# A two-layer conditioned transformer on one core: another order of the work in layer 1's attention, and in the turn from MLP 0 into it

## The chip, the cores and the metric

One Trainium2 chip, one of its cores. The metric is the device time of one execution in microseconds (us); the kernel before has a median of 254.11 us over 3 runs (253.97 to 254.25).

## The reference, cut to what matters

128 sequences of 32 rows, 128 features, float32. Two layers, each an attention and an MLP (128 to 512 to 128, exact gelu), both conditioned on a vector per sequence. Layer 0 has 16 heads, a layernorm, and a gate per sequence on what each half adds to the rows. Layer 1, which the change is about, has one head:

```python
h = film(rmsnorm(x, norm1_w), cond, film1_w, film1_b)     # x * (1 + scale) + shift, per sequence
Q, K, V = h @ q_w + q_b, h @ k_w + k_b, h @ v_w + v_b
attn = softmax(einsum("bnd,bmd->bnm", Q, K) * D ** -0.5)
x = x + (einsum("bnm,bmd->bnd", attn, V) @ proj_w + proj_b)
x = x + mlp(film(rmsnorm(x, norm2_w), ...))
```

The last step of MLP 0 is `x = x + gate_mlp * h`.

## The kernel before, in words

The 4096 rows lie as 32 tiles of 128 rows in the tile `X` of the on-chip memory. The work goes in 8 groups (`NG`) of 4 tiles: a group is 512 rows, 16 whole sequences. There are four phases of 8 groups: attention 0, MLP 0, attention 1, MLP 1. A running number `gg = phase * 8 + g` names a group in a phase: 16 to 23 are attention 1, 24 to 31 MLP 1. Most buffers are double and are picked by `p = g % 2`.

The order on each engine is written out by hand, a list per engine; the engines meet by counting semaphores (`wait_ge(sem, n)`), and each engine works its own list strictly in order. `group_steps` writes a step for the first one or two groups, then a hardware loop of two groups a turn, then the rest.

The chain of one group `gg` before its products:

- the statistics: in attention 1 ScalarE squares the rows (`sum_squares`), GpSimd raises to the power -1/2 (`power1`, L459) and scales the rows (`scale_rows`, L452) into `xhat`. For group 18, and in the MLPs, VectorE makes the statistics, GpSimd `power` (L338, L340) and ScalarE `apply` (L818).
- `rows_T` on TensorE (L1032) transposes 4 tiles of `xhat` into a PSUM bank; `modulate` on VectorE (L555) multiplies by the scale into `hA`; `add_shift` on GpSimd (L351) adds the shift into `h`. In attention 1 this last one also waits until the scores of the group two back are done (`s1_ready`), since these read the same buffer.

The products of group g of attention 1 on TensorE: `queries1` (L1282, h times the folded q/k matrix), `rows1` (L1288, V with the projection folded in, and a column of row terms), `scores1` (L1297, 16 products of 32 columns), `values1` (L1313, P times V into `y_ps`). Between them ScalarE moves the queries (`move_q1`, L1004) and takes the exponentials (`exps1`, L984); VectorE takes maxima and biases (`softmax1`, L650 to L655), moves V (`move_v1`, L674), divides and transposes P (`normalise1`, L660, L662, L667) and adds the product to the rows (`update(2, g)`, L567). `update(2, 0)` waits until `x_updated` is 17, which is reached when MLP 0's last group has been added to its rows.

MLP 0's group g ends so: `down` (L1275, 32 matmuls) into `y_ps`; VectorE adds the bias (`update(1, g)`, L564) into the single tile `yG`; GpSimd multiplies by the gate (L374) and adds to `X` (L376), both in `add_gated`. The product of MLP 0's last group, `down(1, 7)`, stands in TensorE's list behind the first products of attention 1.

TensorE's order before, in attention 1 (numbers are groups):

```
g = 0:     queries 0, rows 0, down(1,7), rows_T 18, scores 0, queries 1
g = 1..7:  rows g, scores g, queries g+1, (wait for P, V of g-1), rows_T g+18, values g-1
```

VectorE's: in a turn `softmax1(g)`, `move_v1(g)`, `modulate(g+18)`, `normalise1(g)`, `update(2, g-1)`. GpSimd's: `scale_rows(g+19)`, `add_shift(g+18)`, `power1(g+20)`, with `add_gated(1, 7)` in the turn of g = 0.

Of the kernel before, what the change touches and what calls it, by code (L numbers as in the profile page):

```python
# [17 lines left out]
ALU = mybir.AluOpType  # L18
ACT = mybir.ActivationFunctionType
# [11 lines left out]
TG = 4  # L31
NG = NT // TG
# [26 lines left out]
def build(nc, x, cond, weights, columns, rows, out):  # L59
    with ExitStack() as ctx:  # L60
# [9 lines left out]
        X = sb("X", [P, NT, D])  # L70
# [33 lines left out]
        eps1 = sb("eps1", [P, 1])  # L104
# [69 lines left out]
        def by_tile(ap):  # L174
            return ap.rearrange("p (t d) -> p t d", t=TG)
# [151 lines left out]
        def _(pool):  # L327
# [35 lines left out]
            def keep(phase, g, p):  # L363
# [2 lines left out]
                wait(pool, x_updated, gg)  # L366
                pool.tensor_tensor(by_tile(xg[:, p, :]), X[:, x_group(g), :], biases(phase), ALU.add).then_inc(xg_ready, 1)

            def add_gated(phase, g):

                gg = phase * NG + g
                pool.wait_ge(y_used, gg + 2)
                at = x_group(g) if isinstance(g, int) else bass.ds((gg + NG) % NG * TG, TG)
                pool.tensor_tensor(by_tile(yG[:, :]), by_tile(yG[:, :]), gate[:, phase, at, :], ALU.mult).then_inc(xg_ready, 1)  # L374
                pool.wait_ge(xg_ready, gg + 1)
                pool.tensor_tensor(X[:, at, :], X[:, at, :], by_tile(yG[:, :]), ALU.add).then_inc(x_updated, 1)  # L376

            def add_shift_half(half):
                if half == 0:
# [64 lines left out]
            def scale_rows(gg, p):  # L444

                pool.wait_ge(rstd_ready, gg + 1)
                if isinstance(gg, int) and gg == 2 * NG + 3:
                    pool.wait_ge(hT_ready, gg)
                else:
                    pool.wait_ge(hT_ready, gg - 1)  # L450
                at = x_group(gg % NG) if isinstance(gg, int) else bass.ds(gg % NG * TG, TG)
                pool.tensor_tensor(by_tile(xhat[:, p, :]), X[:, at, :],  # L452
                                   rstd[:, p, :].unsqueeze(2).broadcast_to([P, TG, D]), ALU.mult).then_inc(xhat_ready, 1)

            def power1(gg, p):

                pool.wait_ge(v_ready, gg + 1)
                wait(pool, xhat_ready, gg - 1)
                pool.tensor_tensor(rstd[:, p, :], v_sb[:, p, :], minus_half[:, :], ALU.pow).then_inc(rstd_ready, 1)  # L459

            def attention1(g, p):
                scale_rows(2 * NG + g + 3, 1 - p)
                add_shift(2 * NG + g + 2, p, 2, g)
                if isinstance(g, int) and g == 0:
                    add_gated(1, 7)
                if known(g, 0, NG - 1):
                    power1(2 * NG + g + 4, p)

            def mlp(phase):
                def step(g, p):  # L470
                    gg = phase * NG + g
                    first = isinstance(g, int) and g == 0
                    if phase == 1 and first:
                        power(gg + 3, 1 - p)
                        add_shift(gg + 2, p, phase, g)
                        pool.wait_ge(gates_in[0], 16 * NG)
                        add_gated(0, 7)
                        return
                    if phase == 1 or known(g, 0, 6):
                        add_shift(gg + 2, p, phase, g)  # L480
                    if phase == 1:
                        power(gg + 3, 1 - p)
                    elif known(g, 0, 5):
                        power(gg + 3, 1 - p, NG)
                    if phase == 1:
                        if p == 1:
                            pool.wait_ge(gates_in[1], 8 * (g + 1))
                        add_gated(1, g - 1)
                    else:
                        keep(phase, g, p)  # L490
                return step

            group_steps(pool, attention0)
            group_steps(pool, mlp(1))
            power1(2 * NG + 3, 1)
            group_steps(pool, attention1, first=2, turns=2)
            group_steps(pool, mlp(3), turns=2)


        @block.vector  # L500
        def _(dve):
# [268 lines left out]
            def attention1(g, p):  # L770
                first = isinstance(g, int) and g == 0
                if first:
                    move_v1(g, p)
                    update(1, 7, 1)
                    modulate(2 * NG + g + 2, p)
                    softmax1(g)
                    normalise1(g, p)
                    return
                softmax1(g)
                move_v1(g, p)  # L780
                modulate(2 * NG + g + 2, p)
                normalise1(g, p)
                update(2, g - 1, 1 - p)

            group_steps(dve, attention0)
            group_steps(dve, mlp(1))
            group_steps(dve, attention1, first=2)
            group_steps(dve, mlp(3), turns=2)
            dve.wait_ge(xg_ready, 3 * NG)
            for half in range(2):  # L790
# [7 lines left out]
        def _(act):  # L798
# [205 lines left out]
                act.activation(Qs[:, p, :], bank[2][:, :], ACT.Identity, bias=wqk[:, D + 1:D + 2]).then_inc(q1_moved, 1)  # L1004

            def attention1(g, p):
                if known(g, 0, NG - 1):
                    sum_squares(2 * NG + g + 4, p, range(TG))
                exps1(g, p)
                if known(g, 0, NG - 1):  # L1010
                    move_q1(g + 1, 1 - p)

            group_steps(act, mlp(1))
            sum_squares(2 * NG + 3, 1, range(TG))
            act.wait_ge(wqk_copied, 1)
            move_q1(0, 0)
            group_steps(act, attention1, first=2, turns=2)
            group_steps(act, mlp(3), turns=2)


        @block.tensor
        def _(pe):
# [299 lines left out]
            def mlp(phase):  # L1322
                def step(g, p):
                    gg = phase * NG + g
                    first = isinstance(g, int) and g == 0
                    if first and phase == 1:
                        rows_T(NG + 2, 0)
                        up(1, 1, 1, (0,))
                        output_T(7, 1)
                        up(1, 1, 1, (1,))  # L1330
                        project0(7, 1)
                        up(1, 1, 1, (2, 3))
                        return
                    elif first:
                        pe.wait_ge(v1_moved, NG)
                        pe.wait_ge(bias1_ready, NG)
                        pe.wait_ge(wmlp1_in, 16)
                        up(phase, g, p)
                    elif not (phase == 1 and isinstance(g, int) and g == 1):
                        up(phase, g, p)  # L1340
                    else:
                        fold_qk()
                    if phase < 3 or not isinstance(g, int) or g < 6:
                        rows_T(gg + 2, p)
                    if not first:
                        down(phase, g - 1, 1 - p)
                    elif phase == 3:
                        wait_values1(7)
                        values1(1)
                return step  # L1350

            def attention1(g, p):
                first = isinstance(g, int) and g == 0
                if first:
                    pe.wait_ge(g_ready, NC * NG)
                    pe.wait_ge(wqk_copied, 1)
                    queries1(g, p)
                rows1(g, p)
                if first:
                    down(1, 7, 1)  # L1360
                    rows_T(2 * NG + g + 2, p)
                scores1(g, p)
                if known(g, 0, NG - 1):
                    queries1(g + 1, 1 - p)
                if not first:
                    wait_values1(g - 1)
                    rows_T(2 * NG + g + 2, p)
                    values1(1 - p)

            group_steps(pe, mlp(1), first=2)  # L1370
            group_steps(pe, attention1, first=2, turns=2)
# [47 lines left out]
```

## Time and profile before

| what | value |
|---|---|
| median of 3 runs | 254.11 us |
| the profiled execution's own time | 254.23 us |
| its span, first to last instruction | 252.4 us |
| TensorE (PE) matmuls busy | 239.5 us, 95% |
| VectorE (DVE) | 162.8 us, 65% |
| ScalarE (ACT) | 156.8 us, 62% |
| GpSimd (POOL) | 154.2 us, 61% |
| mean granted TensorE clock | 0.999 |
| attention 0, with the start | 0 to about 96 us |
| MLP 0 | about 96 to 153.7 us |
| attention 1 | 153.7 to 189.1 us |
| MLP 1 | 189.1 to 252.4 us |

PE is busy in nearly the whole span, so the time is that of PE's list plus the holes in it. Float32 products go through PE in passes, so `queries1` shows as 2 matmuls and `rows1` as 8. The profile's own 1.8 us between span and time lie around the program.

### The profile page before, as it was taken

Reading aid. Unit: us, or ns where it says so; the run is one execution under the profiler, and the core shown is the slowest. Engines: PE = TensorE matmul, PEld = TensorE weight load, DVE = VectorE, ACT = ScalarE, POOL = GpSimd, SP = SyncE. Lnnn points to the kernel's source line nnn. Section 1 sums busy time; section 2 is a strip of 40 time slices with the busy share of each in tenths; the row PEclk is TensorE's granted clock in tenths of the full one; section 3 lists DMA queues with packets and bytes.
Section 4 is the critical chain, followed back from the end, with each engine's and each line's share of the span. In section 5 each row is a group of like instructions: output and inputs, shape, how many; then the busy total and the mean of one; then the engine's idle time right before and its main releaser. Section 6 shows DMA issues by size and latency. Waiting matters only on the chain.

```text
span 252.4 us, 9860 instructions
## 1 busy us (share of the span) xinstructions
PE 239.5 (95%) x3727; PEld 181.0 (72%) x3727; DVE 162.8 (65%) x507; ACT 156.8 (62%) x396; POOL 154.2 (61%) x173
## 2 busy tenths in 40 slices
PE   5899879999999989999999999899999999999995
PEld 5676667787877866766778669677775766677775
DVE  7898888988989997455554543578888354442102
ACT  5469867866966849745445666887856666443340
POOL 4486846585685778677656667788784544554120
PEclk9999999999999999999999999999999999999999
DMA  6943334325256222412100000000000011110112
GB/s 192 326 127 91 122 128 116 122 65 164 94 145 206 104 76 71 134 62 75 71 12 0 0 0 0 4 3 4 0 4 0 0 44 42 42 29 14 44 42 83
DMA packets 17163, 18.01 MB, mean 71 GB/s; under 512 B 1648, under 2 KB 12656, under 8 KB 17136
## 3 DMA queue, kind: packets, MB, share of 16 engines
q1 hardware_dynamic: 16272, 15.41, 20.0%
q10 hardware_dynamic: 864, 2.24, 2.8%
q8 instruction: 17, 0.28, 0.6%
q14 instruction: 10, 0.08, 0.1%
HBM read 11.48 MB, written 4.59 MB: 64 GB/s over the span
## 4 chain that ended last, share of the span: by engine, by line
PE 80%; DVE 4%; POOL 4%; issue 4%; DMA 2%; SPq 2%; ACT 2%; POOLq 0%; ACTq 0%; DVEq 0%
PE bank L1275 23%; PE bank L1064 10%; PE pair L1064 10%; PE bank L1032 5%; PE bank L1142 5%; PE pair L1112 4%; PE bank L1124 3%; PE bank L1163 3%; PE pair L1288 3%; PE pair L1079 2%; PE bank L1071 2%; PE bank L1282 2%; PE bank L1313 2%; PE bank L1112 2%; PE bank L1092 2%
## 5 line engine op out<-in xcount | busy, mean ns | idle before, releaser
L818 ACT ACTIVATE xhat<-X,shift,rstd 128x128 f32 (+1 forms) x88 | 36.9, 487 | 41.1 <-POOL shift L340 41.1
L1275 PE MATMUL bank<-W,Kx 128*128 128x128 f32 x512 | 59.6, 275 | 0.0
L1275 PEld LDWEIGHTS bank<-W,Kx 128*128 128x128 f32 x512 | 58.5, 192 | 1.0 <-issue 1.0
L351 POOL TENSOR_TENSOR h<-hA,B 128x512 f32<-128x512 f32 x31 | 32.5, 1048 | 32.6 <-DVE hA L555 32.4
L555 DVE TENSOR_TENSOR hA<-bank,A 128x512 f32<-128x512 f32 x31 | 21.1, 681 | 32.9 <-PE bank L1032 17.7
L1064 PE MATMUL bank<-h,W 128*128 128x512 f32 x62 | 32.0, 597 | 0.1
L338 POOL TENSOR_TENSOR rstd<-v_sb,minus_half 128x4 f32<-128x4 f32 x24 | 24.5, 1020 | 10.9 <-DVE v_sb L540 5.8
L1064 PE MATMUL pair<-h,W 128*128 128x512 f32 x62 | 29.4, 592 | 0.0
L359 POOL TENSOR_TENSOR Ss<-Sc,smax 128x512 f32<-128x512 f32 x16 | 16.8, 1050 | 18.9 <-DVE smax L581 18.8
L896 ACT ACTIVATE Kx<-bank,col 128x512 f32<-128x512 f32 x32 | 21.7, 677 | 8.1 <-PE bank L1064 8.1
L1032 PEld LDWEIGHTS bank<-ident,xhat 128*128 128x128 f32 x124 | 15.0, 142 | 14.8 <-issue 12.9
L374 POOL TENSOR_TENSOR yG<-yG,gate 128x512 f32<-128x512 f32 x16 | 20.3, 1271 | 7.9 <-DVE yG L564 6.8
L376 POOL TENSOR_TENSOR X<-X,yG 128x512 f32 (+1 forms) x16 | 20.4, 1272 | 2.4 <-POOL yG L374 2.1
L873 ACT ACTIVATE Sc<-bank 128x512 f32<-128x512 f32 x16 | 9.6, 599 | 19.0 <-PE bank L1112 18.1
L1064 PEld LDWEIGHTS pair<-h,W 128*128 128x128 f32 x62 | 11.5, 190 | 13.4 <-issue 13.4
L896 ACT ACTIVATE Kx<-pair,col 128x512 f32<-128x512 f32 x32 | 20.3, 676 | 0.7 <-PE pair L1064 0.7
L526 DVE BATCH_NORM_STATS2 stats<-X 128x6 f32 (+1 forms) x96 | 20.6, 277 | 0.1
L1032 PE MATMUL bank<-ident,xhat 128*128 128x128 f32 x124 | 18.9, 275 | 0.5 <-ACT xhat L818 0.3
L564 DVE TENSOR_TENSOR yG<-bank,row 128x512 f32<-128x512 f32 x16 | 10.8, 676 | 11.9 <-PE bank L1275 9.2
L1142 PE MATMUL bank<-Vx,PT 128*32 128x36 f32 x1024 | 14.8, 200 | 3.8 <-DMA Kx<-Ks 1.2
L1142 PEld LDWEIGHTS bank<-Vx,PT 128*32 128x32 f32 x1024 | 12.2, 109 | 8.6 <-issue 5.5
L1112 PE MATMUL bank<-Kx,Qs 32*32 32x128 f32 x512 | 18.2, 273 | 0.0
(155 smaller groups left out, 467.3 us busy)
## 6 DMA issues: line engine op xcount, KB each, us to landing
values_scratch<-Vs SPq DMA_DIRECT2D x8, 288.0 KB, 2.1
Vx<-values_scratch SPq DMA_DIRECT2D x32, 72.0 KB
gate<-gates_scratch SPq DMA_DIRECT2D x8, 256.0 KB
gate<-gates_scratch SPq DMA_DIRECT2D x4, 512.0 KB
out<-X SPq DMA_DIRECT2D x7, 256.0 KB, 2.3
Kx<-Ks SPq DMA_DIRECT2D x24, 64.0 KB, 2.3
X<-x SPq DMA_DIRECT2D x4, 256.0 KB, 5.5
W<-weights ACTq DMA_DIRECT2D x1, 640.5 KB, 3.8
```

Of the source, the lines that this page charges most:

```text
L338: pool.tensor_tensor(rstd[:, p, :], v_sb[:, p, :], minus_half[:, :], ALU.pow).then_inc(pool_chain, 1)
L351: pool.tensor_tensor(by_seq(h[:, p, :]), by_seq(hA[:, p, :]), B[:, seqs(gg)].unsqueeze(2).broadcast_to([P, GB, L]), ALU.add).then_inc(h_re ...
L376: pool.tensor_tensor(X[:, at, :], X[:, at, :], by_tile(yG[:, :]), ALU.add).then_inc(x_updated, 1)
L526: last = dve.bn_stats(stats[:, t, :], X[:, x_tile(gg, t), :])
L555: dve.tensor_tensor(by_seq(hA[:, p, :]), by_seq(hT_ps[:, :]), A[:, seqs(gg)].unsqueeze(2).broadcast_to([P, GB, L]), ALU.mult).then_inc(hA_ ...
L818: last = act.activation(xhat[:, p, P * t:P * (t + 1)], X[:, x_tile(gg, t), :], ACT.Identity, bias=shift[:, p, t:t + 1], scale=rstd[:, p, t ...
L896: act.activation(gT[:, p, n, :], bank[2 + n][:, :], ACT.Gelu, bias=bias).then_inc(g_ready, 1)
L1032: last = pe.transpose(hT_ps[:, P * t:P * (t + 1)], xhat[:, p, P * t:P * (t + 1)], ident[:, :])
L1064: last = pe.matmul(bank[2 + n][:, :], w(f"W1_{phase // 2}", n), h[:, p, :], start=True, stop=True)
L1112: last = pe.matmul(bank[4 + odd(b)][at:at + L, P * (b % TB):P * (b % TB + 1)], Qs[rows_of, p, L * b:L * (b + 1)], Kx[rows_of, p, :, L * b: ...
L1142: last = pe.matmul(to, PT[:, odd(b), from_:from_ + L], Vx[:, p, :, at_v(b, n):at_v(b, n) + VW], start=True, stop=True)
L1275: last = pe.matmul(y[t // 2][:, P * t:P * (t + 1)], gT[:, p, n, P * t:P * (t + 1)], w(f"W2_{phase // 2}", n), start=(n == 0), stop=(n == N ...
```

## The change

It rewrites the order of attention 1 on four engines; no product is added or dropped.

- **TensorE.** A turn becomes `rows_T g+18`, `queries g`, `rows g`, (wait for P, V of g-1), `scores g`, `values g-1`: queries are no longer made a group ahead, and scores and values stand together. Group 0: queries 0, rows 0, `rows_T 18`, then `down(1, 7)`, scores 0. Group 1: queries 1, rows 1, `rows_T 19`, scores 1, values 0. In MLP 1's first step the wait for V and biases stands behind the first chunk of `up`.
- **VectorE.** `update(2, g-1)` comes before `normalise1(g)`, and `modulate` is last in a turn and of the next group (g+19). In group 0: `move_v1`, `modulate(18)`, `softmax1(0)`, `update(1, 7)`, `normalise1(0)`, `modulate(19)`. The loop has 2 turns and not 3.
- **ScalarE.** `move_q1(0)` comes ahead of both `sum_squares`, and an exponential of one column stands ahead of attention 1.
- **GpSimd.** `add_gated` is cut into `times_gate` and `add_to_rows`. Behind MLP 0: `add_shift(18)`, then `power1(19)`, `scale_rows(19)`. Group 0: `power1(20)`, `times_gate(1, 7)`. Group 1: `scale_rows(20)`, `add_shift(19)`, `power1(21)`, `add_to_rows(1, 7)`. In MLP 1's first step `power(27)` comes ahead of `add_shift(26)`.

```diff
             def attention1(g, p):            # GpSimd
-                scale_rows(2 * NG + g + 3, 1 - p)
-                add_shift(2 * NG + g + 2, p, 2, g)
-                if isinstance(g, int) and g == 0:
-                    add_gated(1, 7)
+                first = isinstance(g, int) and g == 0
+                if not first:
+                    scale_rows(2 * NG + g + 3, 1 - p)
+                    add_shift(2 * NG + g + 2, p, 2, g)
                 if known(g, 0, NG - 1):
                     power1(2 * NG + g + 4, p)
+                if first:
+                    times_gate(1, 7)
+                if isinstance(g, int) and g == 1:
+                    add_to_rows(1, 7)
...
             group_steps(pool, mlp(1))
+            add_shift(2 * NG + 2, 0, 2, 0)
             power1(2 * NG + 3, 1)
+            scale_rows(2 * NG + 3, 1)
...
                 if first:                    # VectorE, attention1
                     move_v1(g, p)
-                    update(1, 7, 1)
                     modulate(2 * NG + g + 2, p)
                     softmax1(g)
-                    normalise1(g, p)
-                    return
-                softmax1(g)
-                move_v1(g, p)
-                modulate(2 * NG + g + 2, p)
+                    update(1, 7, 1)
+                else:
+                    softmax1(g)
+                    move_v1(g, p)
+                    update(2, g - 1, 1 - p)
                 normalise1(g, p)
-                update(2, g - 1, 1 - p)
+                if known(g, 0, NG - 1):
+                    modulate(2 * NG + g + 3, 1 - p)
...
             group_steps(act, mlp(1))
-            sum_squares(2 * NG + 3, 1, range(TG))
             act.wait_ge(wqk_copied, 1)
             move_q1(0, 0)
+            sum_squares(2 * NG + 3, 1, range(TG))
+            sum_squares(2 * NG + 4, 0, range(TG))
+            act.activation(warm[:, :], eps1[:, :], ACT.Exp)
...
                     queries1(g, p)           # TensorE, attention1, g = 0
+                    rows1(g, p)
+                    rows_T(2 * NG + g + 2, p)
+                    down(1, 7, 1)
+                    scores1(g, p)
+                    return
+                if isinstance(g, int) and g == 1:
+                    queries1(g, p)
+                    rows1(g, p)
+                    rows_T(2 * NG + g + 2, p)
+                    scores1(g, p)
+                    wait_values1(g - 1)
+                    values1(1 - p)
+                    return
+                rows_T(2 * NG + g + 2, p)
+                queries1(g, p)
                 rows1(g, p)
-                if first:
-                    down(1, 7, 1)
-                    rows_T(2 * NG + g + 2, p)
+                wait_values1(g - 1)
                 scores1(g, p)
-                if known(g, 0, NG - 1):
-                    queries1(g + 1, 1 - p)
-                if not first:
-                    wait_values1(g - 1)
-                    rows_T(2 * NG + g + 2, p)
-                    values1(1 - p)
+                values1(1 - p)
```

## Rows read from the trace of the kernel before

**Rows 1.** The page: the span, and busy time by engine.
```profile
span 252.4 us, 9860 instructions
PE 239.5 (95%) x3727; PEld 181.0 (72%) x3727; DVE 162.8 (65%) x507; ACT 156.8 (62%) x396; POOL 154.2 (61%) x173
```

**Rows 2.** Windows of attention 1: length, busy us (instructions) PE, PEld, DVE, ACT, POOL, clock.
```profile
159.50:167.40 7.90, 6.99 (x152) 4.79 (x152) 5.41 (x18) 7.03 (x37) 7.61 (x8) 1.00 0.01 3
167.40:183.40 16.00, 15.99 (x313) 11.78 (x313) 13.00 (x36) 12.75 (x73) 12.56 (x13) 1.00 0.01 3
192.80:198.70 5.90, 5.62 (x50) 2.99 (x49) 2.16 (x6) 3.04 (x7) 3.44 (x4) 1.00 0.00 0
```

**Rows 3.** Chain that ended last, in order of time: start, us, what; entry and one turn.
```profile
153.72 0.86 PE bank L1282 x2
154.58 0.89 PE pair L1288 x8
155.47 3.57 PE bank L1275 x32
...
168.53 0.44 PE bank L1032 x4
168.97 1.00 PE bank L1313 x32
169.97 1.09 PE pair L1288 x8
171.06 0.39 PE bank L1297 x32
171.45 1.05 PE bank L1282 x2
```

**Rows 4.** The same chain where attention 1 passes into MLP 1.
```profile
189.09 1.06 PE bank L1064 x2
190.14 1.72 PE pair L1064 x4
191.86 0.87 PE bank L1064 x2
...
198.07 0.65 PE bank L1032 x4
198.72 3.57 PE bank L1275 x32
```

**Rows 5.** Timeline of POOL: start, us, line, operation, shapes, idle before.
```profile
160.63 1.05 POOL L351 TENSOR_TENSOR h<-hA,B 128x512 f32<-128x512 f32 x1
161.63 1.27 POOL L374 TENSOR_TENSOR yG<-yG,gate 128x512 f32<-128x512 f32 x1
162.98 1.27 POOL L376 TENSOR_TENSOR X<-X,yG 128x512 f32<-128x512 f32 x1
164.21 1.01 POOL L459 TENSOR_TENSOR rstd<-v_sb,minus_half 128x4 f32<-128x4 f32 x1
165.31 1.04 POOL L452 TENSOR_TENSOR xhat<-X,rstd 128x512 f32<-128x512 f32 x1
...
193.96 1.05 POOL L351 TENSOR_TENSOR h<-hA,B 128x512 f32<-128x512 f32 x1 [3.52 <-DVE hA L555]
```

**Rows 6.** Timeline of DVE, the end of one turn.
```profile
165.41 0.17 DVE L660 RECIPROCAL rden<-den 128x4 f32<-128x4 f32 x1
...
165.94 0.31 DVE L667 STREAM_TRANSPOSE PT<-Pn 128x128 f32<-128x128 f32 x1
166.17 0.65 DVE L567 TENSOR_TENSOR X<-bank,X 128x512 f32<-128x512 f32 x1
```

**Rows 7.** Timeline of ACT, the exponentials and the queries of one turn.
```profile
168.12 0.26 ACT L984 ACTIVATE bank<-bank,bias 128x32 f32<-128x32 f32 x1 [0.65 <-DVE bias L655]
...
169.09 0.21 ACT L984 ACTIVATION_READ_ACCUMULATOR bank<-bank,bias 128x1 f32 x1
169.19 0.70 ACT L1004 ACTIVATE Qs<-bank,wqk 128x512 f32<-128x512 f32 x1
```

More of the change, by code:

```diff
@@ L367, in keep, with gated_at, times_gate, add_to_rows @@
                 pool.tensor_tensor(by_tile(xg[:, p, :]), X[:, x_group(g), :], biases(phase), ALU.add).then_inc(xg_ready, 1)
-            def add_gated(phase, g):
[L371 to L376, printed above, removed]
+            def gated_at(g):
+                return x_group(g) if isinstance(g, int) else bass.ds((g + NG) % NG * TG, TG)
+            def times_gate(phase, g):
+                pool.wait_ge(y_used, phase * NG + g + 2)
+                pool.tensor_tensor(by_tile(yG[:, :]), by_tile(yG[:, :]), gate[:, phase, gated_at(g), :],
+                                   ALU.mult).then_inc(xg_ready, 1)
+            def add_to_rows(phase, g):
+                at = gated_at(g)
+                pool.wait_ge(xg_ready, phase * NG + g + 1)
+                pool.tensor_tensor(X[:, at, :], X[:, at, :], by_tile(yG[:, :]), ALU.add).then_inc(x_updated, 1)
+            def add_gated(phase, g):
+                times_gate(phase, g)
+                add_to_rows(phase, g)
             def add_shift_half(half):
@@ L478, in step @@
                         return
+                    if phase == 3 and first:
+                        power(gg + 3, 1 - p, NG)
                     if phase == 1 or known(g, 0, 6):
@@ L482, in step @@
                         power(gg + 3, 1 - p)
-                    elif known(g, 0, 5):
+                    elif not first and known(g, 0, 5):
                         power(gg + 3, 1 - p, NG)
@@ L773, in attention1 @@
                     move_v1(g, p)
-                    update(1, 7, 1)
                     modulate(2 * NG + g + 2, p)
                     softmax1(g)
-                    normalise1(g, p)
-                    return
-                softmax1(g)
-                move_v1(g, p)
-                modulate(2 * NG + g + 2, p)
+                    update(1, 7, 1)
[3 more added lines that the diff above has]
+                    update(2, g - 1, 1 - p)
                 normalise1(g, p)
-                update(2, g - 1, 1 - p)
+                if known(g, 0, NG - 1):
+                    modulate(2 * NG + g + 3, 1 - p)
             group_steps(dve, attention0)
             group_steps(dve, mlp(1))
-            group_steps(dve, attention1, first=2)
+            group_steps(dve, attention1, first=2, turns=2)
             group_steps(dve, mlp(3), turns=2)
@@ L1006, in attention1 @@
             def attention1(g, p):
-                if known(g, 0, NG - 1):
+                if known(g, 1, NG - 1):
                     sum_squares(2 * NG + g + 4, p, range(TG))
@@ L1334, in step @@
                     elif first:
+                        pe.wait_ge(wmlp1_in, 16)
+                        up(phase, g, p, (0,))
                         pe.wait_ge(v1_moved, NG)
                         pe.wait_ge(bias1_ready, NG)
-                        pe.wait_ge(wmlp1_in, 16)
-                        up(phase, g, p)
+                        up(phase, g, p, (1, 2, 3))
                     elif not (phase == 1 and isinstance(g, int) and g == 1):
@@ L1357, in attention1 @@
                     queries1(g, p)
+                    rows1(g, p)
[13 more added lines that the diff above has]
+                queries1(g, p)
                 rows1(g, p)
-                if first:
-                    down(1, 7, 1)
-                    rows_T(2 * NG + g + 2, p)
+                wait_values1(g - 1)
                 scores1(g, p)
-                if known(g, 0, NG - 1):
-                    queries1(g + 1, 1 - p)
-                if not first:
-                    wait_values1(g - 1)
-                    rows_T(2 * NG + g + 2, p)
-                    values1(1 - p)
+                values1(1 - p)
             group_steps(pe, mlp(1), first=2)
```

## The prediction

> **What bounds the kernel now.** The page comes first: the matmuls are busy for 239.5 of 252.4 us, and no other engine passes 65% [rows 1]. The time is therefore the length of PE's list plus its holes. The windows of the stage that the change touches come next. Four turns of attention 1 fill 16.00 us, PE is busy for 15.99 of them, DVE for 13.00, ACT 12.75, POOL 12.56 [rows 2]: PE sets the turn, but the others have only 0.75 to 0.86 us a turn to spare. The entry, 159.5 to 167.4, is another matter: PE is busy for 6.99 of 7.90 us and POOL for 7.61 [rows 2]. There POOL is the fullest engine. The chain in order of time gives what each product costs. In a turn: transposes 0.44, values 1.00, rows 1.09, scores 0.39, queries 1.05, together 3.97 us [rows 3]. In the entry the same queries take 0.86 and the same rows 0.89 [rows 3]. So a product on the whole array costs 0.19 to 0.20 more right behind one on small tiles (rows behind values, queries behind scores). There are two such seams in a turn.
>
> **PE's turn.** The new order is transposes, queries, rows, scores, values. Scores and values stand together, so one seam is left, values to transposes. I price it as the seam from values to rows, 0.20: 0.64 + 0.86 + 0.89 + 0.39 + 1.00 = 3.78, or 0.19 less than now. The passage from scores to values is new. It lies between nothing (it stays among small tiles) and one seam (0.20), and I take nothing, since the seams seen are all from small tiles to the whole array. Bounds of a turn: 3.58 with no seam at all, 3.98 with two. The Trainium skill (TensorE: Matmul & The Clock Gate, Step-by-step) says that weight loads are pulled ahead of running matmuls where row groups don't conflict or the load goes to the background buffer. Taken to hold at every seam it would make the turn 3.58; rows 3 speak against that, for there the seam costs 0.2 twice.
>
> Can the others hold 3.78? Busy time a turn is 3.25 on DVE, 3.19 on ACT, 3.14 on POOL [rows 2], unchanged by the edit. The new ring is scores, maximum and bias, exponentials, division and transpose of P, `modulate`, next maximum: 0.39, some 0.7 for three small DVE instructions (an estimate, at the 0.17 of the reciprocal each and the gaps), 1.18 (168.12 to 169.30, rows 7), 0.84 (165.41 to 166.25, rows 6), 0.65 as for the addition of the same size (rows 6). But the scores don't stand in DVE's own round, 0.7 + 1.18 + 0.84 + 0.65 = 3.4. That fits. Queries are now made in the same turn as their scores: ACT's 0.70 [rows 7] plus two hand-overs must fit behind the rows' 0.89, with some 0.05 to spare. I add 0.03 a turn: 3.81.
>
> **The entry: POOL's list.** This is the term that decides. What PE does ahead of scores 0 is the same in another order: 0.86 + 0.89 + 0.44 + 3.57 from 153.72, so scores 0 begin at 159.48 and end 0.39 later, at 159.87 [rows 3], as they did. Transposing 18 early gives `modulate(18)` early, but `add_shift(18)` also waits for scores 0, because it overwrites what these read. It gains nothing, yet it has been moved to the head of POOL's list, ahead of `power1(19)` and `scale_rows(19)`, which before were done by the time shift 18 began (160.63, rows 5). So from about 160.0, with 0.1 for the hand-over, POOL works nine instructions in a row: shift 18 1.05, power 19 1.01, scale 19 1.04, power 20 1.01, gate 1.27, scale 20 1.04, shift 19 1.05, power 21 1.01, add to rows 1.27 [rows 5], together 9.75. The start-to-start times in rows 5 agree: 161.63 to 162.98 to 164.21 to 165.31. The last one, `add_to_rows(1, 7)`, ends at 169.75; before, it ended at 164.25 [rows 5].
>
> Who waits for it: `update(2, 0)` on DVE needs that count. Before, it ran at 166.17 [rows 6] and found it there. Now it stands in DVE's list ahead of `normalise1(1)` and `modulate(20)`. DVE stands from about 165.8 to 169.8, then update 0.65, division and transpose 0.84 [rows 6]: P of group 1 is ready at 171.4 with two hand-overs. PE's new order has the wait for this P ahead of scores 2. Until then PE has holes anyway: transposes 19 wait for POOL's scale 19 (163.1), transposes 20 for scale 20 (166.5), then queries and rows of group 2 are done by 168.9. Scores 2 begin at 171.4; values 1 end at 171.4 + 0.39 + 1.00 = 172.8. Before, values 1 ended at 169.97 [rows 3]. Lost so far: 2.85 us.
>
> **From there to MLP 1's first `down`.** Before: 169.97 to 198.72 [rows 3, 4], 28.75 us. After: five turns of 3.81 = 19.05; `up` 24 1.06 + 1.72 + 0.87 = 3.65 [rows 4]; transposes 26 0.44; values 7 1.00; `up` 25 3.65; transposes 27 0.44. That is 28.25. It holds queries 3, which before had already been made, and so the saving is only 0.5: five times 0.16 for the seam in a turn, 0.1 for turn 7, which kept a seam, 0.45 at the exit (189.09 to 198.72 is 9.63 us for the same products that sum to 9.18, since xhat 27 came late and transposes 27 took 0.65, [rows 4]; `power(27)` ahead of `add_shift(26)` mends that), less 0.86 for queries 3. MLP 1 is PE's alone behind that and moves as a whole.
>
> **Edits at no cost.** `move_q1(0)` early: scores 0 wait for `down`, not for it. The extra exponential of one column: the table load that it draws falls between the squares and the first biases, where the exponentials drew it before. The later wait for V in `up`: it saves nothing as PE is late there. DVE's loop of 2 turns: the same instructions. No DMA is touched; the output's begin some 2 us later with the rows they carry.
>
> **Sum.** +2.85 - 0.5 = +2.35 us on the profiled execution, 254.23 to 256.6; that execution is 0.12 above the median, so 256.4 for the median.
>
> **Rivals.**
>
> *A, the forecast (0.74):* POOL's row of nine ends the wait before scores 2, the turn falls to about 3.8. 256.4.
>
> *B, the turn doesn't fall (0.15):* a seam from scores to values, or the late queries, keep the turn at 3.98. For it: only 0.05 us stands between queries, their move and the scores. Against it: busy times. Then 5 x 0.17 more: 257.3; with 0.1 more a turn from a ring through DVE and ACT, 257.8.
>
> *C, the other side: POOL's row is short (0.05).* Its place is 160.0 to 169.75. DVE stands still for two fifths of it, and if POOL's instructions are long only beside DVE's work, they shrink. It decides from 2.35 us less in nine, a mean of 0.82 instead of 1.08. At DVE's 0.65 for 128x512 in the six long ones and 1.01 in the three powers the row is 6.9 us, scores 2 begin 2.8 us earlier, and the time is 253.6. Against it: POOL's shift takes 1.05 at 193.96 behind 3.5 us without POOL work and 1.05 at 160.63 in the full entry [rows 5]. The Trainium skill (GPSIMD Engine Reference, Key points) has such a rule: GpSimd shares its memory interfaces with VectorE and is held up by instructions with two operands from that memory. The equal rows speak against a weight here.
>
> *D, the whole of it hides (0.02):* scores 2 begin late but the turns that follow catch up. It needs a turn of 3.3, and the five products alone sum to 3.58. 254.1.
>
> *E, the clock falls (0.04):* PE has three holes, about 1.4, 1.5 and 2.5 us, within 10 us. The granted clock was 1.00 in every window shown, the entry with 0.9 us of holes among them [rows 2]. At 1.2 GHz a turn's products take twice as long; one such turn adds 3.8: 260.2.
>
> **How the numbers follow.** Low end: every seam gone (turn 3.58 instead of 3.81, -1.15) and a POOL row 2% shorter (-0.2) gives 255.1. High end: turn 3.98 and 0.1 for the ring, with 0.2 for hand-overs in the entry, 258.0. Outside stay C, D, E and some of both tails. A measurement of this kernel can tell 0.2%, 0.5 us. Faster: C's larger part, 0.04. Same: D and the rest of C, 0.03. Slower: 0.93.
>
> **What would show it.** Right: POOL's addition to the rows at about 168.5; DVE's update of group 16 behind some 4 us of idle time with that addition as releaser; PE's idle time before scores 2 of about 2.5 us; scores 3 to 7 some 3.8 us apart; MLP 1's first `down` at 200.9 to 201.1. Wrong on the turn: scores 4.0 apart. Wrong on the entry: the addition before 167, or scores 2 that wait for something else, say rows 2 or the transposes 20.

## The result, and the profile after

The changed kernel has a median of 258.34 us over 5 runs (257.39 to 258.96); the kernel before 254.25 us in the same comparison (253.97 to 254.93). The ratio is 1.0143, with a 95% interval of 1.0119 to 1.0168: slower by 3.6 us (3.0 to 4.3). The ratio on the 254.11 us of the front gives 257.7, inside the forecast range (255.1 to 258.0) at its upper end; the plain median of the five, 258.34, lies 0.3 us above the range. Ratios are of fast runs alone: a run more than 1.5% above the fastest of its kernel counts as slow and is left out. The profiled execution took 258.34 us, its span 256.5 us, 4.1 more than before.

First, the windows of the changed kernel around the passage from MLP 0 to attention 1, with the columns of [rows 2]:

```profile
169.50:171.50 2.00, 0.00 (x0) 0.00 (x0) 1.43 (x5) 1.01 (x7) 1.40 (x2) 1.00 0.00 0
171.50:173.00 1.50, 1.22 (x44) 1.13 (x48) 0.98 (x3) 0.00 (x0) 0.35 (x1) 0.58 0.05 11
173.00:175.00 2.00, 2.00 (x32) 1.54 (x21) 1.27 (x3) 1.19 (x8) 1.76 (x3) 0.50 0.00 0
175.00:177.00 2.00, 2.00 (x13) 1.40 (x11) 1.59 (x5) 0.79 (x3) 0.95 (x1) 0.96 0.00 0
```

Two things are to be seen. From 169.5 to 171.5 PE does nothing at all. And right behind this hole the column of the granted clock reads 0.58 and 0.50, half of 2.4 GHz, where it read 1.00 in all of [rows 2].

Second, GpSimd's timeline in the changed kernel, the row of nine:

```profile
160.34 1.05 POOL L351 TENSOR_TENSOR h<-hA,B 128x512 f32<-128x512 f32 x1 [3.05 <-PE bank L1319]
161.35 1.02 POOL L471 TENSOR_TENSOR rstd<-v_sb,minus_half 128x4 f32<-128x4 f32 x1
162.45 1.04 POOL L464 TENSOR_TENSOR xhat<-X,rstd 128x512 f32<-128x512 f32 x1
163.44 1.01 POOL L471 TENSOR_TENSOR rstd<-v_sb,minus_half 128x4 f32<-128x4 f32 x1
164.42 1.27 POOL L376 TENSOR_TENSOR yG<-yG,gate 128x512 f32<-128x512 f32 x1
165.65 1.04 POOL L464 TENSOR_TENSOR xhat<-X,rstd 128x512 f32<-128x512 f32 x1
166.64 1.05 POOL L351 TENSOR_TENSOR h<-hA,B 128x512 f32<-128x512 f32 x1
167.65 1.01 POOL L471 TENSOR_TENSOR rstd<-v_sb,minus_half 128x4 f32<-128x4 f32 x1
168.64 1.26 POOL L383 TENSOR_TENSOR X<-X,yG 128x512 f32<-128x512 f32 x1
```

It waits 3.05 us for scores 0 (L1319), then works without a gap to 169.90. Before, shift 18 began 0.3 us later, but the addition to the rows began at 162.98 [rows 5].

Third, who waits for it: VectorE, then TensorE (timelines of DVE and PE):

```profile
170.00 0.69 DVE L587 TENSOR_TENSOR X<-bank,X 128x512 f32<-128x512 f32 x1 [3.90 <-POOL X L383]
...
171.14 0.31 DVE L687 STREAM_TRANSPOSE PT<-Pn 128x128 f32<-128x128 f32 x1
```

```profile
163.54 0.66 PE L1054 MATMUL bank<-ident,xhat 128*128 128x128 f32 x4 [1.35 <-POOL xhat L464]
...
166.82 0.65 PE L1054 MATMUL bank<-ident,xhat 128*128 128x128 f32 x4 [1.22 <-POOL xhat L464]
...
171.78 0.66 PE L1319 MATMUL bank<-h,Qs 128*32 128x32 f32 x32 [2.56 <-DVE PT L687]
172.37 1.93 PE L1335 MATMUL bank<-Vs,PT 32*32 32x128 f32 x32
```

DVE stood 3.90 us with the addition as its releaser, PE 2.56 us with P of group 1 as its own. The two holes before transposes 19 and 20 are GpSimd's as well.

Fourth, the chain in order of time, from scores 2 to MLP 1's first `down` (start, us, what):

```profile
171.78 0.66 PE bank L1319 x32
172.44 1.86 PE bank L1335 x32
174.30 1.02 PE bank L1054 x4
175.32 0.86 PE bank L1304 x2
176.18 0.89 PE pair L1310 x8
177.07 0.39 PE bank L1319 x32
177.46 1.01 PE bank L1335 x32
178.46 0.59 PE bank L1054 x4
179.05 0.86 PE bank L1304 x2
179.91 0.89 PE pair L1310 x8
180.80 0.39 PE bank L1319 x32
...
202.41 0.44 PE bank L1054 x4
202.85 3.24 PE bank L1297 x29
```

The turn is shorter: 177.07 to 180.80 is 3.73 us, against 3.97 in [rows 3]. And three products ran at the low clock: scores 2 took 0.66 instead of 0.39, values 1 1.86 instead of 1.00, transposes 21 1.02 instead of 0.59, together 1.56 us.

Not every execution has this. The mean granted clock of the five executions was 0.993 in three (258.34, 258.71, 258.96 us) and 1.000 in the other two (257.39, 257.85 us). The profiled one is of the first kind.

The same program does not reach scores 0 at the same moment in each execution: from 159.2 to 161.6 in the profiles of this study, most of which arises ahead of queries 0, where TensorE's list was not edited. So kernels are compared below by the **length from the start of scores 0 to the start of MLP 1's first `down`**: 159.41 to 198.72 before, 39.31 us; 159.70 to 202.85 changed, 43.15 us, which is 3.84 more. One edit lies outside it: transposes 18 now stand ahead of `down(1, 7)`. From queries 0 to scores 0 TensorE took 5.85 us before and 6.05 after (timelines, the kernel before first):

```profile
153.56 1.02 PE L1282 MATMUL bank<-h,wqk 128*128 128x512 f32 x2
...
159.41 0.46 PE L1297 MATMUL bank<-h,Qs 128*32 128x32 f32 x32
```

```profile
153.65 1.02 PE L1304 MATMUL bank<-h,wqk 128*128 128x512 f32 x2
...
159.70 0.46 PE L1319 MATMUL bank<-h,Qs 128*32 128x32 f32 x32
```

All kernels with the new order have this 0.20 us (6.05 or 6.06), and e5, which has the old one, 5.86. Counted from queries 0 the changed kernel is thus 4.04 us longer; the other 0.1 of the 4.1 arose ahead of it.

| kernel | length, us | ratio to before | interval |
|---|---|---|---|
| before | 39.31 | 1 | |
| changed | 43.15 | 1.0143 | 1.0119 to 1.0168 |
| e1: power and scale 19 first | 41.37 | 1.0046 | 1.0014 to 1.0079 |
| e2: gated sum whole | 41.73 | 1.0082 | 1.0050 to 1.0113 |
| e3: GpSimd early | 37.22 | 0.9897 | 0.9847 to 0.9947 |
| e4: changed, with filler | 41.87 | 1.0092 | 1.0057 to 1.0127 |
| e5: exit alone | 38.82 | 0.9981 | 0.9961 to 1.0001 |
| e6: e3, P first | 37.22 | 0.9898 | 0.9866 to 0.9929 |
| e7: changed, chain cut | 40.82 | 1.0069 | 1.0046 to 1.0093 |
| e8: e1, with filler | 39.81 | 1.0016 | 0.9993 to 1.0039 |
| e9: e6, scores 2 first | 37.69 | 0.9948 | 0.9929 to 0.9967 |
| e10: e3, turns written out | 37.69 | 0.9927 | 0.9899 to 0.9955 |
| e11: e9, looped | 37.18 | 0.9910 | 0.9880 to 0.9939 |
| e12: e4, looped | 41.38 | 1.0083 | 1.0054 to 1.0113 |

### The profile page after: what moved, and what is told of

The parts are those of the page before. It is cut to its first block, busy times and chain, and to the rows that moved or that the text cites. A ratio compares the mean times of both kernels' runs of the same rounds, so it can differ in the third digit from the quotient of the medians.

```text
span 256.5 us, 9846 instructions
## 1 busy us (share of the span) xinstructions
PE 240.0 (94%) x3727; PEld 182.8 (71%) x3727; DVE 162.9 (63%) x507; ACT 157.7 (61%) x397; POOL 154.1 (60%) x173
## 4 chain that ended last, share of the span: by engine, by line
PE 83%; issue 3%; POOL 3%; DMA 3%; DVE 3%; ACT 2%; SPq 2%; POOLq 0%; DVEq 0%; ACTq 0%
PE bank L1297 22%; PE bank L1086 11%; PE pair L1086 10%; PE bank L1054 5%; PE bank L1164 5%; PE pair L1134 4%; PE bank L1335 3%; PE bank L1146 3%; PE bank L1185 3%; PE pair L1101 2%; PE bank L1093 2%; PE pair L1310 2%; PE bank L1304 2%; PE bank L1134 2%; PE bank L1058 2%
## 5 line engine op out<-in xcount | busy, mean ns | idle before, releaser
L1054 PE MATMUL bank<-ident,xhat 128*128 128x128 f32 x124 | 19.7, 283 | 2.7 <-POOL xhat L464 2.6
L1134 PE MATMUL pair<-Kx,Qs 32*32 32x128 f32 x512 | 17.3, 271 | 0.5 <-issue 0.5
```

Source lines behind the costliest of these rows:

```text
L1054: last = pe.transpose(hT_ps[:, P * t:P * (t + 1)], xhat[:, p, P * t:P * (t + 1)], ident[:, :])
L1134: last = pe.matmul(bank[4 + odd(b)][at:at + L, P * (b % TB):P * (b % TB + 1)], Qs[rows_of, p, L * b:L * (b + 1)], Kx[rows_of, p, :, L * b: ...
```

## The experiments

They are told in the order in which they bear on each other; e5 to e8 ran after e1 to e4, and e9 to e12 after these. The theory has two parts. **P**: the chain from GpSimd's row of nine over `update(2, 0)` and P of group 1 to scores 2 is the entry's price. **K**: PE's hole before scores 2 also brought the clock down. The rival **R**: the new turn itself, with its wait for P ahead of the scores, costs the time.

**e1, two of the nine taken out of the row.**

```diff
             group_steps(pool, mlp(1))
-            add_shift(2 * NG + 2, 0, 2, 0)
             power1(2 * NG + 3, 1)
             scale_rows(2 * NG + 3, 1)
+            add_shift(2 * NG + 2, 0, 2, 0)
```

> The changed kernel with one thing moved: GpSimd does power 19 and scale 19 ahead of add_shift(18), in the time in which it waits for scores 0. Theory P (GpSimd's row of nine behind scores 0 ends the wait of update(2, 0), and this the wait before scores 2): two of the nine, 2.05 us, leave the row, so the addition to the rows ends near 167.9 instead of 169.9, scores 2 begin near 169.7 instead of 171.8, and the kernel is 2.0 us faster than the changed one, about 256.0. Theory K (the hole before scores 2 also brought the clock down, some 1.5 us): the holes before transposes 19 and 20 are shorter, the last stays near 2.6 us with much PE work ahead of it; if the clock stays up, another 1.5 us less, about 254.4. Rival R (the wait for P ahead of the scores, a ring through three engines, costs the time in every turn, wherever GpSimd stands): no change, 257.9.

Measured: 256.52 us, 1.0046 of before. The timeline of GpSimd has the addition 2.11 us earlier, and the timeline of PE the scores 2.00:

```profile
166.53 1.27 POOL L383 TENSOR_TENSOR X<-X,yG 128x512 f32<-128x512 f32 x1
```

```profile
169.78 0.46 PE L1319 MATMUL bank<-h,Qs 128*32 128x32 f32 x32 [2.65 <-DVE PT L687]
170.17 1.89 PE L1335 MATMUL bank<-Vs,PT 32*32 32x128 f32 x32
```

The length is 1.78 us shorter than the changed kernel's, where 2.0 was expected. P holds within 0.3; R, which foresaw no change, falls. The hole stayed (2.65) and the clock fell behind it again: values 1 took 1.82 us in the chain, transposes 21 1.05 and queries 3 1.21. So the "another 1.5 us less", which the expectation had for a clock that stays up, did not come.

**e2, the gated sum whole again.**

```diff
                 if first:
-                    times_gate(1, 7)
-                if isinstance(g, int) and g == 1:
-                    add_to_rows(1, 7)
+                    add_gated(1, 7)
```

> The changed kernel with the gated sum whole again: multiplication and addition together in the turn of group 0. Theory P: the addition ends at 167.1, update(2, 0) no longer holds P of group 1, but scale 20 comes 1.27 us later, and transposes 20 with it. Scores 2 then wait for PE's own list, 168.2 + 0.64 + 0.86 + 0.89, near 170.7, 1.1 us earlier than in the changed kernel. The hole of 2.6 us before scores 2 is gone and the one before transposes 20 grows from 1.2 to some 2.5 us. If K is right and the clock falls behind a long hole, it can fall here too, earlier; if it does 256.8, if it doesn't 255.3. Rival R: 257.9.

Measured: 257.14 us, 1.0082. The length is 1.42 us shorter. PE's timeline:

```profile
167.64 1.11 PE L1052 MATMUL bank<-ident,xhat 128*128 128x128 f32 x4 [2.57 <-POOL xhat L464]
168.54 1.91 PE L1302 MATMUL bank<-h,wqk 128*128 128x512 f32 x2
...
171.31 0.46 PE L1317 MATMUL bank<-h,Qs 128*32 128x32 f32 x32
```

The hole moved from scores 2 to transposes 20, where it lasts 2.57 us, and the low clock moved with it: transposes 1.11 instead of 0.66, queries 1.91 instead of 1.02. The case "if it does" of the expectation came about. The cut of the sum in two parts cost about 1.4 us here, since its second half ended up behind three more instructions, with DVE waiting.

**e3, GpSimd's order made early.**

```diff
             group_steps(pool, mlp(1))
-            add_shift(2 * NG + 2, 0, 2, 0)
             power1(2 * NG + 3, 1)
             scale_rows(2 * NG + 3, 1)
+            power1(2 * NG + 4, 0)
+            add_shift(2 * NG + 2, 0, 2, 0)
+            scale_rows(2 * NG + 4, 0)
+            add_gated(1, 7)
```

In the turns of groups 0 and 1 these are left out; nothing else differs from the changed kernel.

> The changed kernel with another order on GpSimd: power 19, scale 19 and power 20 ahead of add_shift(18), then scale 20, the whole gated sum, add_shift(19), power 21. Only shift 18, scale 20, gate and addition, 4.6 us, stand behind scores 0 and ahead of update(2, 0). Theory P: no wait before transposes 19 and 20, addition done near 165.5, scores 2 near 167.4 where the kernel before had them at 167.0 with queries 3 still ahead of them now. With turns of 3.75 and the shorter exit, MLP 1's first down begins near 197.1, 1.6 us ahead of the kernel before: 252.6, faster than both. K: no hole above 1 us, so the clock stays at full. Rival R: the turns cost more than before wherever GpSimd stands, and the time is at least that of the kernel before, 254.3 or more.

Measured: 252.68 us, 0.9897 of before. It beats both kernels; e6 and e11 below are its equals within their intervals. GpSimd's timeline:

```profile
159.64 1.01 POOL L471 TENSOR_TENSOR rstd<-v_sb,minus_half 128x4 f32<-128x4 f32 x1
160.61 1.05 POOL L351 TENSOR_TENSOR h<-hA,B 128x512 f32<-128x512 f32 x1
...
163.97 1.27 POOL L383 TENSOR_TENSOR X<-X,yG 128x512 f32<-128x512 f32 x1
```

PE's chain in order of time:

```profile
167.17 0.46 PE bank L1319 x29
167.63 1.01 PE bank L1335 x32
```

Scale 19 and power 20 now fill the time in which GpSimd waited for scores 0. The addition ends at 165.24, scores 2 begin at 167.17, and the length is 2.09 us below that of before. PE's order, TensorE's wait for P ahead of the scores and all turns are those of the changed kernel: R is refuted from the other side.

**e4, filler in the hole.** In group 2, ahead of the wait, with the groups 2 and 3 written out instead of looped, and 4 and 5 in a loop of one turn (`first=4, turns=1`):

```diff
                 rows1(g, p)
+                if isinstance(g, int) and g == 2:
+                    for n in range(20):
+                        pe.transpose(bank[5][:, 2 * P:3 * P], ident[:, :], ident[:, :])
                 wait_values1(g - 1)
```

> The changed kernel with 20 transposes of the identity, 2.2 us of PE work without use, in the hole of 2.6 us before scores 2. They put nothing on the path. Theory K (the clock fell because PE stood still in that hole, and the fall costs 0.27 on scores 2, 0.86 on values 1 and 0.4 on transposes 21): the clock stays at full, the addition of GpSimd still ends at 169.9, scores 2 still begin near 171.8, and the kernel is 1.5 us faster than the changed one, about 256.4. Rival (those products are long for another reason, as the passage from scores to values): no change, 257.9.

Measured: 257.62 us, 1.0092 of before, where the changed kernel had 1.0143; the intervals overlap narrowly (up to 1.0127 and from 1.0119). The length differs more clearly: 41.87 against 43.15, 1.28 us less. Timeline of PE:

```profile
169.43 2.35 PE L1399 MATMUL bank<-ident 128*128 128x128 f32 x20
171.96 0.46 PE L1319 MATMUL bank<-h,Qs 128*32 128x32 f32 x32 [0.19 <-DVE PT L687]
172.35 1.07 PE L1335 MATMUL bank<-Vs,PT 32*32 32x128 f32 x32
```

P of group 1 is ready as long behind scores 0 as in the changed kernel (11.8 us), so GpSimd's chain is untouched. But scores 2 follow it at once, where they came 0.32 us behind it in the changed kernel, and values 1 take 1.07 and not 1.93. The clock column reads 1.00 from 168 to 176 us: with work without use in place of rest it stayed up. The gain is smaller than the 1.56 us of the three slow products alone; e10 and e12 below find why.

**e8, the same filler in e1.** It is e1 with e4's lines.

> The kernel with power 19 and scale 19 ahead of add_shift(18), plus the 20 transposes without use in its hole before scores 2. A second measurement of theory K, in a kernel whose hole lies 2 us earlier: without filler the clock fell behind it, and values 1, transposes 21 and queries 3 took 1.82, 1.05 and 1.21 us instead of 1.00, 0.59 and 0.86. With filler the clock stays up: 1.6 us less than that kernel, about 1.002 to 0.998 of the kernel before, 254.6. Rival (the fall has to do with something else than PE's rest): no change, 1.0046 of the kernel before.

Measured: 255.27 us, 1.0016 (e1 had 1.0046; the intervals overlap); the length is 1.56 us below e1's (39.81 against 41.37). That is 1.83 us less up to scores 3, and 0.27 more in the turns behind, on which e10 bears. The window over the hole, the filler and what follows:

```profile
168.00:172.00 4.00, 3.81 (x73) 3.53 (x75) 2.10 (x6) 2.15 (x10) 2.71 (x3) 1.00 0.02 4
```

The column of the clock reads 1.00; in e1 it was 0.57 in the two us behind the hole:

```profile
170.00:172.00 2.00, 2.00 (x64) 1.57 (x48) 1.25 (x4) 0.90 (x7) 1.54 (x2) 0.57 0.03 8
```

Twice, then, rest of 2.6 us was followed by the low clock and work in its place was not.

The executions that left no trace say the same, with less certainty. The mean granted clock is on record for each. It was 0.993 or less in 3 of 5 executions of the changed kernel, 8 of 10 of e1 and 8 of 10 of e2; in the three kernels with filler (e4, e8, e12) in 1 of 26; in the kernel before in 4 of 91. So the hole makes the fall likely and not certain, and the fall can come without it. Within one kernel, executions with the fall were longer on the mean by 1.05 us (changed, 258.67 against 257.62), 1.03 (e1) and 1.56 (e2).

**e7, the chain cut and GpSimd left alone.** DVE divides P of group 1 ahead of `update(2, 0)`; TensorE does scores 2 ahead of the wait.

```diff
+                elif isinstance(g, int) and g == 1:     # VectorE
+                    softmax1(g)
+                    move_v1(g, p)
+                    normalise1(g, p)
+                    update(2, g - 1, 1 - p)
...
+                if isinstance(g, int) and g == 2:       # TensorE
+                    scores1(g, p)
+                    wait_values1(g - 1)
+                    values1(1 - p)
+                    return
```

> The changed kernel, GpSimd's order untouched (nine in a row, addition done at 169.9), but the chain behind the addition is cut: VectorE does normalise1(1) ahead of update(2, 0), and TensorE does scores 2 ahead of the wait for P and the rows of group 1. Theory P (the price is the chain addition, update(2, 0), division and transpose, scores 2, and not GpSimd's row as such): scores 2 begin near 169.1, values 1 near 170.8, where the changed kernel had 171.8 and 172.4. Theory K: the hole is cut in two short ones, the longest 1.3 us, and the clock stays up. Together 2.5 us less than the changed kernel, 255.4. If the clock falls all the same, 256.7. Rival R (GpSimd's fullness itself limits the entry): 257.9.

Measured: 256.64 us, 1.0069; the length is 2.33 us below the changed kernel's. Timeline of PE:

```profile
170.76 1.08 PE L1341 MATMUL bank<-Vs,PT 32*32 32x128 f32 x32 [1.31 <-DVE X L587]
```

Scores 2 began at 168.99 already. The longest hole is 1.34 us and the clock read 1.00 throughout. The expectation was 2.5 less and 255.4: the length agrees within 0.2, the median lies 1.2 above, in runs from 255.9 to 257.5 and one of 260.3. The 2.33 us hold both parts of the theory, the chain and the clock. GpSimd's row is untouched here, so it is the chain behind it that cost, not its fullness.

**e5, the exit alone.** The kernel before with `power(27)` ahead of `add_shift(26)`, as in the change.

> The kernel before with one part of the change alone: in MLP 1's first step GpSimd does power 27 ahead of add_shift(26). Theory: xhat 27 then comes in time, transposes 27 don't wait and cost 0.44 instead of 0.65, and MLP 1's first down begins some 0.5 us earlier, at 198.2 where it began at 198.72. 253.7 where the kernel before has 254.2. Rival: the wait only moves, as add_shift(26) is now 1.2 us later and up 26 or its transposes wait for it: no change.

Measured: 254.50 us, 0.9981 (0.9961 to 1.0001); the length is 0.49 us shorter, as priced (0.45). In the chain, transposes 27 cost 0.44 and not 0.65 [rows 4]:

```profile
198.78 0.44 PE bank L1034 x4
199.22 3.57 PE bank L1277 x32
```

**e6, e3 with P of group 1 ahead of `update(2, 0)`** (e7's VectorE lines alone).

> The kernel with GpSimd's early order, and in VectorE's turn of group 1 normalise1(1) ahead of update(2, 0), so that P of group 1 doesn't stand behind the gated sum. Theory P: the last hole of the entry, 0.69 us before scores 2, falls to 0.1 to 0.2, and the kernel takes 252.1 where the one without this takes 252.7. Rival: update(2, 0) and the scale of group 20 come later by 0.8 us and bring the hole back before scores 2 or transposes 21: 252.7.

Measured: 252.63 us, 0.9898, and the same length as e3, 37.22. The rival was right. The hole stays at 0.63 us, and only its releaser changes, since the wait ahead of the scores also asks for the rows of group 0:

```profile
167.75 0.46 PE L1325 MATMUL bank<-h,Qs 128*32 128x32 f32 x32 [0.63 <-DVE X L587]
```

**e9, e6 with e7's TensorE lines as well.**

> The kernel with GpSimd's early order and normalise1(1) ahead of update(2, 0), and now also scores 2 ahead of the wait for P and the rows of group 1. Theory P: what is left of the entry's price is the chain addition, update(2, 0), values 1. Scores 2 fill 0.4 us of the hole of 0.6, and every later product begins 0.4 us earlier: scores 0 to MLP 1's first down 36.7 us instead of 37.1, the time 252.2. Rival: TensorE gets back to another wait (transposes 21 on the scale of group 20, which VectorE makes later) and nothing changes: 252.6.

Measured: 253.26 us, 0.9948; the length is 37.69, 0.47 longer than e6's. A miss. PE now waits 0.66 us at transposes 21, for scale 21 on GpSimd; but that hole only replaces the one of 0.63. The 0.47 came from the turns behind it: 3.89 us each, where e3's had 3.73. e4, e7 and e8 have the same 3.89, and what these four share is `first=4, turns=1` in TensorE's list: groups 2 and 3 are written out, so that something could be put into group 2, and groups 4 and 5 stand in a loop of one turn.

**e10, the control: e3 with nothing but that.**

```diff
-            group_steps(pe, attention1, first=2, turns=2)
+            group_steps(pe, attention1, first=4, turns=1)
```

> A control. The early-GpSimd kernel, of which only TensorE's list is written down otherwise: groups 2 to 5 as straight code instead of in the loop, the same instructions in the same order. In the kernels with filler or with a changed group 2 these groups were written out too, and their turns took 3.89 us (with 0.08 us between rows and scores) where the looped ones took 3.73. Theory W (straight code itself costs about 0.16 a turn): the length from scores 0 to MLP 1's first down is 37.7 to 37.9 us instead of 37.2, and the time some 253.3. Rival (those kernels are ahead of the other engines and their turn is a ring's): 37.2 and 252.7.

Measured: 252.77 us, 0.9927, and a length of 37.69, 0.47 more than e3's. Theory W holds for the length; the median moved by less than it foresaw, and its interval overlaps e3's. PE's timeline, scores 3 and 4:

```profile
171.35 0.46 PE L1319 MATMUL bank<-h,Qs 128*32 128x32 f32 x32
...
175.24 0.46 PE L1319 MATMUL bank<-h,Qs 128*32 128x32 f32 x32
```

3.89 us apart, where e3 has 3.73, for the same instructions in the same order. All of it lies between the start of the rows and the start of the scores: 1.14 us against 0.98. The same split runs through all kernels with the new order. From group 3 on it is 0.98 to 1.08 us in groups that stand in a loop of two turns, and 1.13 to 1.15 in all others, groups 4 and 5 of e10 among them. "Straight code" in the expectation is thus not exact: a loop of a single turn cost the same as code written out. And group 2 of e7, e9 and e11 is written out too, but has its scores ahead of the wait for P and of the other counts; there it is 0.99. So the 0.16 us were seen only where this wait stands between the rows and the scores.

**e11, e9 with groups 3 to 6 in the loop** (`first=3, turns=2`).

> The kernel with GpSimd's early order, P of group 1 ahead of update(2, 0) and scores 2 ahead of the wait, now with group 2 alone written out and groups 3 to 6 in the loop. Theory W: its miss of 0.47 us was the price of straight code, so three or four turns of 3.73 come back and the length is near 37.1; 252.6. Rival: the wait of transposes 21 for GpSimd was the whole of the miss, 37.7 and 253.2.

Measured: 252.58 us, 0.9910, length 37.18. W again, and what the cut chain itself is worth in the early order comes out as nothing (37.22 in e6).

**e12, e4 with groups 3 to 6 in the loop.**

> The changed kernel with the 20 filler transposes ahead of scores 2, with group 2 alone written out. Theory K with W: the clock's whole price, 1.56 us in products and 0.27 in a late start of scores 2, comes back without the price of straight code, so the length is 41.3 to 41.4 instead of 43.15 in the changed kernel and 41.87 in the first one with filler; about 1.0075 of the kernel before. If W is wrong 41.87.

Measured: 256.86 us, 1.0083. The length is 41.38, in the band that was forecast. PE's timeline, scores 2:

```profile
171.54 0.46 PE L1319 MATMUL bank<-h,Qs 128*32 128x32 f32 x32 [0.20 <-DVE PT L687]
```

The length is 43.15 - 41.38 = 1.77 us below the changed kernel's, and the ratio's interval ends at 1.0113, below the 1.0119 at which that kernel's begins. 1.65 us of the 1.77 lie between scores 0 and scores 3 (15.65 against 17.30): this is the price of the clock in the changed kernel's profiled execution, the late start of scores 2 included. The other 0.12 lie in the turns behind, where e12 has one group fewer outside the loop. In e4 the first part is 1.59 and the turns behind take back 0.31.

## Why the prediction was right or wrong

- **The entry's main chain: right.** Scores 2 were forecast 11.9 us behind the start of scores 0; measured 12.08. The row of nine took 9.56 us (forecast 9.75), DVE's wait 3.90 (4), PE's holes 1.35, 1.22 and 2.56 (1.4, 1.5, 2.5). e1 and e7 each undo a part of it and give back about what it was priced at (1.78 of 2.0; 2.33 of 2.5, the clock included), and e3 comes out at 252.68 where 252.6 was expected.
- **Ahead of scores 0: 0.20 us too low.** The forecast took TensorE's work there as the same in another order. It took 6.05 us and not 5.85, for transposes 18 between rows 0 and `down`.
- **The clock: the step that failed.** Rival E got 0.04, on the ground that the clock was 1.00 in every window read, "the entry with 0.9 us of holes among them". The forecast's own holes came to 5.4 us, so those rows showed nothing like it. The fall came in the profiled executions of the changed kernel, of e1 and of e2, each time with a hole of 2.6 us, and in 19 of these kernels' 25 executions. Its price was mis-sized too, the other way: 1.65 us by e12 (1.83 by e8; 1.0 to 1.6 between executions of one kernel), not a turn at half speed and 3.8. With it the sum would have been 2.35 + 1.65 = 4.0; from queries 0 to the first `down` the profiled execution grew by 4.04. That `down` was forecast at 200.9 to 201.1 and began at 202.85.
- **PE's turn: right.** Forecast 3.81 (3.78 from rows); measured 3.73 in the looped turns and 3.89 in the last two, which are written out. That the mean of the four from scores 3 to scores 7 is 3.81 as well is luck: no row showed the forecast the difference between the two kinds. Scores to values cost nothing (values 1.01), as taken. The seam from values to transposes was priced 0.20 and measured 0.15 (0.59 against 0.44). The rule on weight loads pulled ahead (the Trainium skill, TensorE: Matmul & The Clock Gate, Step-by-step) would have made it nothing; the trace shows that a seam from small tiles to the whole array is left.
- **From values 1 to the first `down`: right in sum.** Forecast 28.25 us, measured 28.55, of which 0.43 is the low clock in transposes 21. e5 shows the exit's 0.49 by itself.
- **Rival C: refuted.** GpSimd's instructions were as long beside a VectorE that stood still (shift 19, 1.05 at 166.64) as beside a busy one. The Trainium skill's rule of shared interfaces (GPSIMD Engine Reference, Key points) names VectorE instructions with two inputs from the shared memory. Beside the nine, each of VectorE's 128x512 instructions read one input from PSUM, so these runs say little of that rule's weight.
- **Rival B: refuted** by the turn, though the written-out turns lose their 0.16 us at the place that it named, between rows and scores. The ring through the other engines that it gave as the cause is not theirs: e10 and e3 have the same ring.
- **The size: inside the range in part by luck.** In the profiled execution the clock accounts for the way from the middle to the upper end. But the range's upper end was built from a longer turn and a ring, and neither came. And the two executions in which the clock did not fall took 257.39 and 257.85 us, still 1.0 to 1.5 us above the 256.4 of the forecast. 0.20 of this is the work ahead of scores 0. Where the rest arose is open, since none of the two left a trace.

## What to carry to other kernels

When a step is moved ahead on an engine that works strictly in order, look first at what it waits for itself: here a step that can't begin before scores 0 was put ahead of two that could, and 2 us of free time behind it were lost. Follow each count that a later step waits for to its last contributor in the new order: half of a sum put behind three other instructions stopped two further engines. And once a forecast has a hole of some us on TensorE, price the clock behind it with the next few products at double length, here three of them and 1.56 us, as a term of the sum and not as a remote case.

## What the runs showed that was not expected

- TensorE's granted clock went from 2.4 to 1.2 GHz (1.00 to 0.50 in the records) at rests of 2.56, 2.57 and 2.65 us, each in a stretch with shorter rests ahead of it. In the profiled executions it did not fall where the longest rest of the stretch was 1.34 us (e7) or where filler stood in the hole (e4, e8, e12). Behind the rest TensorE worked without a pause, and the column read 1.00 again from 177 us on (changed), 174 (e1) and 172 (e2). These runs don't tell whether the one long rest or the sum of rests counts, nor why the same kernel has executions with the fall and without it.
- Filler products of no use made the changed kernel's length 1.77 us shorter (e12) and e1's 1.56 (e8). They don't beat taking the hole away: e3 is 4.16 us below e12.
- The same list of TensorE took 3.89 us a turn written out or in a loop of one turn, and 3.73 in the hardware loop of two turns (e10 against e3, e11 against e9, e12 against e4). The 0.16 us lie between the start of the rows and the start of the scores, and only where the wait for P stands there. Why the loop of two turns is spared is open.
- A new order for GpSimd, on which the bounding engine's time hung only through two others, was worth 5.93 us of length between the changed kernel and e3, in which PE's list is the same instruction for instruction.
